# Weighing six of the twelve context chunks of a batch by three fp32r products of halves instead of plain fp32

## The chip, the cores and the metric

The kernel runs on one core of one Trainium2 chip. Its time is the device time of one execution in microseconds (us): the median of three runs. The page and the rows below come from one further execution that the hardware profiler recorded. The engines are named as in the profile: PE is TensorE, DVE is VectorE, ACT is ScalarE, POOL is GpSimd, SP issues the DMAs.

## What is computed

One decoder layer on `x` (32 batches, 56 tokens, 128 wide), in three parts: a position attention whose weights come from a small LSTM, a cross attention to `ctx_1024` (32 batches, 1500 rows, 128 wide), and a feed-forward layer with four experts. The change lies in the cross attention:

```
def _L0_xattn_ref(Q, K, V, WQ, WK, WV, WO, bO):      # K = V = ctx_1024, 16 heads of 64
    q = (Q @ WQ).reshape(N, ql, HEADS, DK)
    k = (K @ WK).reshape(N, kl, HEADS, DK)
    v = (V @ WV).reshape(N, kl, HEADS, DV)
    compat = jnp.einsum('nqhk,nlhk->nhql', q, k) / math.sqrt(DK)
    weights = jax.nn.softmax(compat, axis=3)
    attn = jnp.einsum('nhqk,nkhv->nqhv', weights, v).reshape(N, ql, HEADS * DV)
    return attn @ WO + bO
```

## The kernel before

WQ with WK, and WV with WO, are folded into one 128x128 matrix a head, so that keys and values are the raw context. A batch has 16 heads x 56 tokens = 896 columns, taken in two halves of 448 (`HALF`), and its 1500 context rows are 12 chunks (`CH`) of 125 (`CR`). Batches go in pairs: `i` is the pair (16), `k` the batch in the pair, `b = 2i + k`.

For chunk `j` of a batch: ACT seeds the PSUM scores with minus the column's maximum (`seed`, L976); PE adds the scores to them by three fp32r products of halves for each 448 columns, high x high, low x high, high x low (`scores`, L717); ACT takes the exponential into `probs[j % 4]` (L1033); POOL adds the chunk into `prob_sum` (L447 for the first two chunks together, L452 for the others); PE weighs the context with it, `ctx_nat` as the stationary operand, in plain fp32 into `usum_ps` (`weigh`, L729). In the trace one plain fp32 product is two matmul instructions, and one fp32r product is one.

The order is written out by hand. PE's `period(i, k)` has 12 slots, one for each `j`. A slot is: scores of chunk j+1, first half; place 0; scores, second half; place 1; weighing of chunk j-1, first half; place 2; weighing, second half; place 3. In the places stands side work, given by the strings `PLACES`, one word a slot (the first row for k = 0, the second for k = 1): m is a 128x500 product for the next batch's column maxima (L598), which DVE reduces (`read_max`, L1252); d spreads the maxima (L603) after DVE has made `max_diag` (L1259); t turns a third of the next context (L590), which ACT and DVE split into halves (L898, L1139); q makes queries (L629); s is the sums (L609) and p the projection (L617) of the previous pair, read by DVE. Side work alternates between two PSUM banks, and a product waits until its bank has been read.

DVE goes through the same slots: `take_u` at j = 1, the reads of place 0, the low halves of turned context (`late_turns`), the reads of place 1, those of places 2 and 3. At j = 11 it makes `q_lo` (L1244) from `q_hi`, which ACT makes just before (`query_hi`, L963). ACT's order for a chunk is: exponential, the copies of side work of slot j-1 (`side_copies`), seed of chunk j+2. The last batch has side work of its own: the layer norm of the third part (L1099, with its power on POOL, L377), routing, and on POOL the halves of the first expert weights (`expert_halves`, L433 and L435).

```
PLACES = ("m..m mssm ssmm mmpm .mpm mmpm mmpm mqmm mqqt ..dd qt.. t...",
          "m..m mm.m mm.m mm.m m.m. m.m. m.mt m.m. m.mt ..dd .... .t..")
```

## Time and profile before

| | |
|---|---|
| median of three runs | 1722.85 us (1722.15 to 1723.15) |
| the profiled execution | 1721.62 us |
| its span, first to last instruction | 1719.5 us |
| PE busy | 1647.4 us, 96% of the span |
| DVE, ACT, POOL busy | 843.5, 918.7, 792.1 us |
| share of the chain that ended last | PE 87%, DVE 8%, ACT 2% |
| mean granted PE clock | 0.975 of full speed |

The chain is the sequence of work that ended last, followed back from the end; a piece of it is what the program really spent, whereas the record of a single matmul also covers the time in which the next is already running behind it. Some 1380 us of the span are the batches' loop, and every pair of batches looks like the one shown below (755.3 to 844.9 us).

### The profile page before, as it was taken

How to read it: one execution, taken by the hardware profiler on the slowest of the kernel's cores; microseconds unless marked ns; L12 is line 12 of the kernel's file. 1: busy time of each engine (PE TensorE's matmuls, PEld its weight loads, DVE VectorE, ACT ScalarE, POOL GpSimd, SP SyncE). 2: the span in 40 equal slices, each digit the busy share in tenths (PEclk: the TensorE clock that was granted, in tenths of full speed). 3: DMA queues.
4: the chain of work that ended last, by engine and by line, in shares of the span. 5: the costliest groups of instructions: out<-in, count | busy, mean ns of one | idle time of the engine just before them, and what ended most of it. 6: DMA issues, size and time to landing. Idle time of an engine off the chain costs nothing.

```text
span 1719.5 us, 25064 instructions
## 1 busy us (share of the span) xinstructions
PE 1647.4 (96%) x7783; PEld 1181.7 (69%) x7783; DVE 843.5 (49%) x1772; ACT 918.7 (53%) x1311; POOL 792.1 (46%) x414
## 2 busy tenths in 40 slices
PE   6876999999999999999999999999999999998997
PEld 3344677777777777777777777767677777776664
DVE  3349445454545444454545445454454545454345
ACT  3233565656565656555555556565656565655211
POOL 2003454545454555545455555454545454545410
PEclk9996899999999999999999999999999999999788
DMA  4000000000000000001010101000000000000000
GB/s 150 25 17 2 1 36 37 36 36 36 36 36 36 36 36 36 36 29 43 18 45 15 44 20 40 31 36 36 36 36 36 36 36 36 36 18 1 1 1 22
DMA packets 15052, 54.84 MB, mean 32 GB/s; under 512 B 919, under 2 KB 6122, under 8 KB 15022
## 3 DMA queue, kind: packets, MB, share of 16 engines
q1 hardware_dynamic: 15022, 54.46, 8.4%
q8 instruction: 17, 0.28, 0.1%
q14 instruction: 13, 0.11, 0.0%
HBM read 53.54 MB, written 0.92 MB: 32 GB/s over the span
## 4 chain that ended last, share of the span: by engine, by line
PE 87%; DVE 8%; ACT 2%; issue 1%; POOL 1%; DMA 0%; DVEq 0%; POOLq 0%; ACTq 0%
PE ps L729 32%; PE ps L717 26%; PE ps L598 9%; PE ps L617 3%; PE ps L629 3%; PE ps L779 3%; PE ps L609 3%; PE ps L590 2%; DVE max_diag L1259 2%; PE ps L524 1%; DVE max_parts L1252 1%; PE ps L603 1%; DVE xnorm L1099 1%; ACT arena L877 1%; ACT arena L880 1%
## 5 line engine op out<-in xcount | busy, mean ns | idle before, releaser
L452 POOL TENSOR_TENSOR arena<-arena,probs 125x896 f32<-125x896 f32 x320 | 677.6, 2118 | 546.8 <-ACT probs L1033 456.6
L729 PE MATMUL ps<-probs,ctx_nat 125*128 125x448 f32 x1536 | 685.7, 544 | 0.0
L1252 DVE TENSOR_REDUCE max_parts<-ps 128x1 f32<-128x500 f32 x672 | 451.6, 676 | 354.7 <-PE ps L598 347.2
L1033 ACT ACTIVATE probs<-ps 125x896 f32<-125x896 f32 x384 | 351.6, 916 | 474.3 <-PE ps L717 430.9
L598 PE MATMUL ps<-ctxT_hi,q_hi 128*128 128x500 f32 x672 | 365.1, 544 | 2.2 <-DVE max_parts L1252 1.3
L976 ACT ACTIVATE ps<-arena 125x896 f32<-125x896 f32 x384 | 354.1, 922 | 7.9
L729 PEld LDWEIGHTS ps<-probs,ctx_nat 125*128 125x128 f32 x1536 | 277.6, 191 | 95.8 <-issue 79.7
L717 PE MATMUL ps<-q_hi,ctxT_hi 128*125 128x448 f32 x768 | 331.2, 431 | 1.8 <-ACT ps L976 1.8
L717 PE MATMUL ps<-q_lo,ctxT_hi 128*125 128x448 f32 x768 | 282.8, 368 | 0.0
L717 PE MATMUL ps<-q_hi,ctxT_lo 128*125 128x448 f32 x768 | 281.7, 367 | 0.0
L717 PEld LDWEIGHTS ps<-q_hi,ctxT_hi 128*125 128x125 f32 x768 | 144.5, 188 | 70.0 <-issue 62.1
L598 PEld LDWEIGHTS ps<-ctxT_hi,q_hi 128*128 128x128 f32 x672 | 127.4, 190 | 82.2 <-DVE max_parts L1252 29.7
L717 PEld LDWEIGHTS ps<-q_lo,ctxT_hi 128*125 128x125 f32 x768 | 144.2, 188 | 42.5 <-issue 22.1
L717 PEld LDWEIGHTS ps<-q_hi,ctxT_lo 128*125 128x125 f32 x768 | 143.2, 186 | 14.2
L447 POOL TENSOR_TENSOR arena<-probs 125x896 f32<-125x896 f32 x32 | 68.4, 2139 | 149.0 <-ACT probs L1033 149.0
L1139 DVE TENSOR_TENSOR ctxT_lo<-ps,ctxT_hi 128x500 fp32r<-128x500 f32 x96 | 64.4, 670 | 131.0 <-ACT ctxT_hi L898 131.0
L1244 DVE TENSOR_TENSOR q_lo<-arena,q_hi 128x896 fp32r<-128x896 f32 x32 | 38.8, 1212 | 92.8 <-ACT q_hi L963 92.8
L898 ACT ACTIVATE ctxT_hi<-ps 128x500 fp32r<-128x500 f32 x96 | 56.3, 587 | 45.9 <-PE ps L590 45.9
L617 PEld LDWEIGHTS ps<-vo_w,arena 128*112 128x112 f32 x512 | 64.0, 176 | 23.8 <-issue 23.8
L1290 DVE SCALAR_TENSOR_TENSOR resid<-ps,sum_recip,resid 112x128 f32 (+1 forms) x128 | 44.3, 346 | 63.6 <-PE ps L617 63.6
L629 PEld LDWEIGHTS ps<-xT,qk_w 128*128 128x128 f32 x512 | 67.1, 196 | 11.0 <-issue 9.1
L629 PE MATMUL ps<-xT,qk_w 128*128 (+1 forms) x512 | 69.3, 281 | 0.6 <-ACT xT L859 0.6
(186 smaller groups left out, 1259.6 us busy)
## 6 DMA issues: line engine op xcount, KB each, us to landing
ctx_raw<-in_ctx_dram SPq DMA_DIRECT2D x32, 750.0 KB
ctx_nat<-in_ctx_dram SPq DMA_DIRECT2D x32, 750.0 KB
w_sb<-in_L_ffn_W_dram SPq DMA_DIRECT2D x1, 1024.0 KB
resid<-in_x_dram SPq DMA_DIRECT2D x1, 896.0 KB, 6.7
out_dram<-ctx_raw SPq DMA_DIRECT2D x4, 224.0 KB, 2.5
ctx_raw<-in_L_xattn_WQ_dram SPq DMA_DIRECT2D x1, 512.0 KB
w_sb<-in_L_xattn_WK_dram SPq DMA_DIRECT2D x1, 512.0 KB
w_sb<-in_L_xattn_WV_dram SPq DMA_DIRECT2D x1, 512.0 KB
```

The lines of the kernel that those rows point to most:

```text
L447: g.tensor_tensor(first_sum if k == 0 else summed, chunk[0], chunk[1], ALU.add).then_inc(s["prob_added"], 1)
L452: g.tensor_tensor(summed, first_sum if j == 2 and k == 0 else summed, chunk[j % NP], ALU.add).then_inc(s["prob_added"], 1)
L598: mm(ps[:, bank, 0:MC], q_hi[nk][:, block_ * 128:(block_ + 1) * 128], ctxT_hi[nk][:, part * MC:(part + 1) * MC], start=True, stop=True).th ...
L617: m = mm(ps[0:TOK, bank, n * D:(n + 1) * D], u_sum[:, h].rearrange("p b q -> p (b q)"), vo_w[:, h, :], start=True, stop=True)
L629: m = mm(ps[:, bank, n * TOK:(n + 1) * TOK], qk_w[:, 4 * which + n, :], xT[:, bass.ds(i + 1, 1), :].rearrange("p k t -> p (k t)"), start=T ...
L717: m = mm(score_ps[j % 2][:, half, :], cx[k][:, rows], q[k][:, cols], start=False, stop=True, skip_group_check=True)
L729: m = mm(usum_ps[:, half, :], ctx_nat[k][:, j, :], probs[j % NP][:, half, :], start=(j == 0), stop=(j == CH - 1))
L898: a(ctxT_hi[k][:, which * MC:(which + 1) * MC], ps[:, bank, 0:MC], ACT.Copy).then_inc(s["ctxT_hi_done"], 1)
L976: a(score_ps[j % 2], neg_max[k][0:CR], ACT.Copy).then_inc(s["seeded"], 1)
L1033: a(probs[j % NP][:], score_ps[j % 2], ACT.Exp, scale=SCALE).then_inc(s["prob_done"], 1)
L1139: v.tensor_tensor(ctxT_lo[k][:, part], ps[:, bank, 0:MC], ctxT_hi[k][:, part].bitcast(F32), ALU.subtract).then_inc(s["ctxT_lo_done"], 1)
L1252: v.tensor_reduce(max_parts[:, which:which + 1], ps[:, bank, 0:MC], AX.X, ALU.max).then_inc(s["max_read"], 1)
```

## The change

Chunks 1, 3, 5, 7, 9 and 11 (`SPLIT`) are weighed by three fp32r products for each 448 columns, `ctx_hi` x `p_hi`, `ctx_hi` x `p_lo`, `ctx_lo` x `p_hi`; the other six stay plain fp32. For this:

- ACT takes a second exponential of the same scores into `p_hi` (fp32r), behind the side copies and ahead of the seed of chunk j+2; the exponential into `probs` stays.
- DVE subtracts, `p_lo = probs - p_hi`, 125x896, between the reads of place 1 and those of places 2 and 3.
- POOL makes `ctx_hi` and `ctx_lo` of the next batch in three parts of two chunks each, behind its adds of chunks 4, 6 and 8: six instructions of 125x256 a batch. The first batch's are made ahead of the loop; in the last batch there are none.
- PE waits for `prob_lo_done` ahead of a split chunk, and for `ctx_lo_done` once a batch.
- `probs` moves into `arena` and `wo_raw`, two of the `onehotT` tiles into `ctx_hi[0]` and `ctx_lo[0]`.

```
+        SPLIT = (1, 3, 5, 7, 9, 11)
...
+            def context_halves(i, k, part):
+
+                nb, (c0, c1) = 2 * i + k, PARTS[part]
+                chunks, halves = slice(c0, c1 + 1, c1 - c0), slice(2 * part, 2 * part + 2)
+                need(pool, f"nat_in{k}", 16 * (i + 1))
+                need(pool, "weighted", CH * (nb - 1))
+                g.tensor_tensor(ctx_hi[k][:, halves, :], ctx_nat[k][:, chunks, :], ones[0:CR, None, :].to_broadcast((CR, 2, D)), ALU.mult).then_inc(s["ctx_hi_done"], 1)
+                need(pool, "ctx_hi_done", len(PARTS) * nb + part + 1)
+                g.tensor_tensor(ctx_lo[k][:, halves, :], ctx_nat[k][:, chunks, :], ctx_hi[k][:, halves, :].bitcast(F32),
+                                ALU.subtract).then_inc(s["ctx_lo_done"], 1)
...
+                    if j in PART_SLOTS and not (isinstance(i, int) and i == PAIRS - 1 and k == 1):
+                        context_halves(i + k, 1 - k, PART_SLOTS.index(j))
...
-                    need(pe, "prob_done", CH * b + j + 1)
-                m = mm(usum_ps[:, half, :], ctx_nat[k][:, j, :], probs[j % NP][:, half, :], start=(j == 0), stop=(j == CH - 1))
+                        need(pe, "ctx_lo_done", len(PARTS) * (b + 1))
+                    if j in SPLIT:
+                        need(pe, "prob_lo_done", split_count(b, j))
+                    else:
+                        need(pe, "prob_done", CH * b + j + 1)
+                if j in SPLIT:
+                    n = SPLIT.index(j)
+                    pairs = ((ctx_hi, p_hi), (ctx_hi, p_lo), (ctx_lo, p_hi))
+                    for m_, (cx, p) in enumerate(pairs):
+                        m = mm(usum_ps[:, half, :], cx[k][:, n, :], p[n % 2][:, half, :], start=(j == 0 and m_ == 0), stop=(j == CH - 1 and m_ == 2))
...
-                    a(probs[j % NP][:], score_ps[j % 2], ACT.Exp, scale=SCALE).then_inc(s["prob_done"], 1)
+                    a(probs[j % NP], score_ps[j % 2], ACT.Exp, scale=SCALE).then_inc(s["prob_done"], 1)
...
+                    if j in SPLIT:
+                        need(act, "weighted", free_half(b, j))
+                        a(p_hi[SPLIT.index(j) % 2], score_ps[j % 2], ACT.Exp, scale=SCALE).then_inc(s["prob_hi_done"], 1)
...
+                    if j in SPLIT:
+                        need(dve, "prob_hi_done", split_count(b, j))
+                        need(dve, "weighted", free_half(b, j))
+                        n = SPLIT.index(j) % 2
+                        v.tensor_tensor(p_lo[n], probs[j % NP], p_hi[n].bitcast(F32), ALU.subtract).then_inc(s["prob_lo_done"], 1)
```

DVE, the end of the batch with k = 1 of the first pair (it is written out ahead of the loop over pairs, in the same order as in the loop), from the maxima of slots 0 to 6 on, before:

```order
L1252 TENSOR_REDUCE max_parts<-ps 128x1 x16
L1139 TENSOR_TENSOR ctxT_lo<-ps,ctxT_hi 128x500
L1252 TENSOR_REDUCE max_parts<-ps 128x1 x3
L1256 TENSOR_REDUCE max_all<-max_parts 128x7
L1259 TENSOR_TENSOR max_diag<-ident,max_all 128x896
L1139 TENSOR_TENSOR ctxT_lo<-ps,ctxT_hi 128x500
L1244 TENSOR_TENSOR q_lo<-arena,q_hi 128x896
```

and after, from the subtraction of chunk 3 on:

```order
L1458 TENSOR_TENSOR p_lo<-wo_raw,p_hi 125x896
L1304 TENSOR_REDUCE max_parts<-ps 128x1 x4
L1458 TENSOR_TENSOR p_lo<-arena,p_hi 125x896
L1304 TENSOR_REDUCE max_parts<-ps 128x1 x4
L1191 TENSOR_TENSOR ctxT_lo<-ps,ctxT_hi 128x500
L1458 TENSOR_TENSOR p_lo<-wo_raw,p_hi 125x896
L1304 TENSOR_REDUCE max_parts<-ps 128x1 x3
L1308 TENSOR_REDUCE max_all<-max_parts 128x7
L1311 TENSOR_TENSOR max_diag<-ident,max_all 128x896
L1191 TENSOR_TENSOR ctxT_lo<-ps,ctxT_hi 128x500
L1458 TENSOR_TENSOR p_lo<-arena,p_hi 125x896
L1458 TENSOR_TENSOR p_lo<-wo_raw,p_hi 125x896
```

The maxima stand as they did; between them, in every odd slot, there is now one subtraction, and the last two of a batch stand around the ninth and eleventh chunk, behind `max_diag` and the turned context.

PE, in the loop at k = 1, a weighing in an even slot with the product for the maxima on either side, before:

```order
L717 MATMUL ps<-q_hi,ctxT_lo 125x448
L213 REGISTER_ALU
L598 MATMUL ps<-ctxT_hi,q_hi 128x500
L729 MATMUL ps<-probs,ctx_nat 128x448 x2
L213 REGISTER_ALU
```

and after, where `L221 ISA` is the wait for `prob_lo_done`:

```order
L634 MATMUL ps<-ctxT_hi,q_hi 128x500
L221 ISA
L773 MATMUL ps<-p_hi,ctx_hi 128x448
L773 MATMUL ps<-p_lo,ctx_hi 128x448
L773 MATMUL ps<-p_hi,ctx_lo 128x448
```

The two plain products (one a half of the columns) have become six, the second three of which read like the first and are left out above; in odd slots the two plain products stay.

## Rows read from the trace of the kernel before

**Rows 1.** The page, busy time, then PE and its clock in 40 slices.

```profile
PE 1647.4 (96%) x7783; PEld 1181.7 (69%) x7783; DVE 843.5 (49%) x1772; ACT 918.7 (53%) x1311; POOL 792.1 (46%) x414
...
PE   6876999999999999999999999999999999998997
...
PEclk9996899999999999999999999999999999999788
```

**Rows 2.** Windows: us, then PE, PEld, DVE, ACT, POOL busy (count), clock, DMA.

```profile
755.30:799.80 44.50, 44.24 (x174) 30.78 (x173) 21.86 (x30) 30.35 (x39) 25.32 (x12) 1.00 0.09 35
799.80:844.90 45.10, 45.10 (x235) 34.91 (x234) 22.28 (x47) 22.58 (x29) 21.24 (x10) 1.00 0.09 34
...
793.90:799.80 5.90, 5.90 (x26) 4.15 (x25) 1.35 (x1) 5.76 (x8) 3.04 (x2) 1.00 0.00 0
...
1559.80:1605.00 45.20, 36.20 (x144) 24.65 (x143) 22.53 (x45) 22.42 (x28) 30.24 (x18) 0.89 0.00 1
```

**Rows 3.** The chain, slot 5 of k = 1: start us, us, what.

```profile
777.04 0.23 PE ps L598
777.26 0.61 PE ps L717 x3
777.87 0.76 PE ps L729 x2
```

**Rows 4.** Groups of instructions: busy us, mean ns of one, idle before and releaser.

```profile
L452 POOL TENSOR_TENSOR arena<-arena,probs 125x896 f32<-125x896 f32 x320 | 677.6, 2118 | 546.8 <-ACT probs L1033 456.6 <-PE ps L609 88.5
```

**Rows 5.** The timeline of DVE: start us, us, instruction, idle before.

```profile
771.55 0.68 DVE L1252 TENSOR_REDUCE max_parts<-ps 128x1 f32<-128x500 f32 x1 [0.17 <-PE ps L598]
...
790.18 2.21 DVE L1259 TENSOR_TENSOR max_diag<-ident,max_all 128x896 fp32r<-128x896 f32 x1
...
798.16 1.35 DVE L1244 TENSOR_TENSOR q_lo<-arena,q_hi 128x896 fp32r<-128x896 f32 x1 [5.18 <-ACT q_hi L963]
...
835.83 1.09 DVE L1259 TENSOR_TENSOR max_diag<-ident,max_all 128x896 fp32r<-128x896 f32 x1
```

**Rows 6.** The timeline of POOL beside it.

```profile
772.47 2.10 POOL L452 TENSOR_TENSOR arena<-arena,probs 125x896 f32<-125x896 f32 x1 [1.38 <-ACT probs L1033]
...
789.33 2.10 POOL L452 TENSOR_TENSOR arena<-arena,probs 125x896 f32<-125x896 f32 x1 [1.33 <-ACT probs L1033]
...
796.46 2.11 POOL L452 TENSOR_TENSOR arena<-arena,probs 125x896 f32<-125x896 f32 x1 [1.63 <-ACT probs L1033]
...
836.58 2.29 POOL L452 TENSOR_TENSOR arena<-arena,probs 125x896 f32<-125x896 f32 x1 [2.34 <-ACT probs L1033]
```

**Rows 7.** The timelines of POOL and DVE in the last batch, where POOL is backlogged.

```profile
1594.43 1.27 POOL L435 TENSOR_TENSOR ctxT_lo<-w_sb,ctxT_hi 128x512 fp32r<-128x512 f32 x1
1595.66 4.36 POOL L452 TENSOR_TENSOR arena<-arena,probs 125x896 f32<-125x896 f32 x2
...
1595.85 1.96 DVE L1314 SCALAR_TENSOR_TENSOR arena<-arena 112x12 f32<-112x12 f32 x1
...
1598.06 2.00 DVE L1314 SCALAR_TENSOR_TENSOR arena<-arena 112x12 f32<-112x12 f32 x1
```

**Rows 8.** The chain around `max_diag` at k = 1, and in the last batch.

```profile
790.18 2.22 DVE max_diag L1259
...
792.54 0.45 PE ps L603
...
795.15 1.50 PE ps L729 x4
796.66 1.22 PE ps L717 x6
...
1566.71 5.42 DVE xnorm L1099 x4
```

**Rows 9.** The timeline of ACT at the end of k = 1.

```profile
794.55 0.92 ACT L976 ACTIVATE ps<-arena 125x896 f32<-125x896 f32 x1
795.41 0.90 ACT L1033 ACTIVATE probs<-ps 125x896 f32<-125x896 f32 x1
```

More of the change, by code:

```diff
@@ L91, in decoder_layer @@
         ctx_nat = [sb(f"ctx_nat{n}", [CR, CH, D]) for n in range(2)]
+        ctx_hi = [sb(f"ctx_hi{n}", [CR, NS, D], F32R) for n in range(2)]
+        ctx_lo = [sb(f"ctx_lo{n}", [CR, NS, D], F32R) for n in range(2)]
         ctxT_hi = [sb(f"ctxT_hi{n}", [D, L], F32R) for n in range(2)]
@@ L95, in decoder_layer @@
         q_lo = [sb(f"q_lo{n}", [D, HQ], F32R) for n in range(2)]
-        probs = [sb(f"probs{n}", [CR, 2, HALF]) for n in range(NP)]
+        p_hi = [sb(f"p_hi{n}", [CR, 2, HALF], F32R)[:] for n in range(2)]
+        p_lo = [sb(f"p_lo{n}", [CR, 2, HALF], F32R)[:] for n in range(2)]
         max_diag = sb("max_diag", [128, HQ], F32R)
@@ L116, in decoder_layer @@
         neg_max = [cut(HQ).rearrange("p (a b) -> p a b", a=2) for n in range(2)]
-        cut(3 * HQ)
+        probs = [cut(HQ, CR).rearrange("p (a b) -> p a b", a=2) for n in range(NP - 1)] + [
+            wo_raw[0:CR].rearrange("p f n -> p (f n)")[:, 0:HQ].rearrange("p (a b) -> p a b", a=2)]
         prob_sum = cut(2 * HQ, CR).rearrange("p (h b q) -> p h b q", h=H, b=2)
@@ L187, in decoder_layer @@
         b1_r = sb("b1_r", [E, 2, FF], F32R)
-        onehotT = [sb(f"onehotT{q}", [E, GT], F32R)[:] for q in range(GROUPS)]
+        spare = NS * D // GT
+        onehotT = [half[0:E].rearrange("p c d -> p (c d)")[:, n * GT:(n + 1) * GT] for half in (ctx_hi[0], ctx_lo[0]) for n in range(spare)]
+        onehotT += [sb(f"onehotT{q}", [E, GT], F32R)[:] for q in range(len(onehotT), GROUPS)]
         xT_halves = max_diag[:].rearrange("p (n t) -> p n t", n=2)
```

21 lines of the change are left out of this document (18 added, 3 removed).

## The prediction

> **What bounds the kernel now.** I read the page first. PE is busy 96% of the span and its clock is granted nine tenths or more in nearly all slices [rows 1]; the reader is to see that PE, at its full clock of 2.4 GHz, fills the loop. The windows over one pair of batches, the first with the batch k = 1 and one slot more, the second with most of k = 0, show it exactly: PE busy 44.24 us of 44.50 and 45.10 of 45.10, while ACT has 30.35 and 22.58, DVE 21.86 and 22.28, POOL 25.32 and 21.24 [rows 2]. So in the loop a nanosecond taken from PE is a nanosecond of the end, as long as nobody else comes late. The last batch is different: PE is busy only 36.20 of 45.20 us there [rows 2], and the chain runs over POOL and DVE [rows 8].
>
> **What one split weighing gives.** The chain gives the real price of each product, free of overlaps. Three fp32r products of 448 columns (the scores, L717) take 0.61 us, also where six of them take 1.22; one plain fp32 weighing of 448 columns (L729, two instructions) takes 0.76, or 0.75 where two of them take 1.50 [rows 3, 8]. Operands, columns and bank type of the new triple are those of the scores, except that the moving operand has 125 partitions and the stationary one 128 columns where the scores have 128 and 125. I take 0.755 - 0.61 = 0.145 us for each half of a chunk. There are 6 chunks x 2 halves x 32 batches = 384 of them: 384 x 0.145 = 55.7 us. Of these 12 lie in the last batch, where PE waits anyway; I count them at nothing: 372 x 0.145 = 53.9 us. Bounds for one half: 0.12 (a triple that costs 0.635, a little over 0.2 us a product) to 0.16.
>
> Against the rows stands a rule. The Trainium skill, "FP8 and Floating Point Precision", section TensorE Precision Notes, says that true FP32 makes four passes through the array. By it the change would save one pass of four, a quarter of 0.755, or 0.19 us a half and 73 us in all; the rows say 0.145, since an fp32r product takes 0.203 us and not 0.189. The sum goes by the rows.
>
> **What it adds, and under what it lies.**
> ACT: one exponential a split chunk, at the pace of one every 0.86 us (0.92 long, starts at 794.55 and 795.41 [rows 9]): 6 x 0.86 = 5.2 us a batch, to 30.35 + 5.2 = 35.5 of some 43 us at k = 1 and 27.8 at k = 0. It lies under PE, except at the end of k = 1, where ACT is already busy 5.76 of 5.90 us [rows 2] and two of the new exponentials (chunks 9 and 11) fall. ACT runs ahead there by more than a microsecond (the seed of the next batch's chunk 0 is done at 795.47, its scores begin at 796.66 [rows 8, 9]), so of 1.7 us more most is covered. Behind the new exponential are queued the seed of chunk j+2 and, at j = 11, `q_hi`; PE waits for both. Price: 0 to 0.6 us a pair; I take 0.1.
> DVE: one subtraction of 125x896 from two SBUF tiles. The nearest row is `max_diag`, 1.09 us, alone [rows 5]: 6 x 1.0 = 6 us a batch, to 28 of some 43. What is queued behind it are the reads of places 2 and 3, and so the banks of PE's side work.
> POOL: six instructions of 125x256. The nearest rows are 1.27 us for 512 columns [rows 7] and 2.12 for 896 [rows 4], on a line through which 256 columns take 0.7: 4.2 us a batch. With that POOL has 29.5 us of some 43 at k = 1. Behind them wait its adds, and for those only the ring of four `probs`, three slots later, and the sums of the next pair.
>
> **The wait that the change adds.** The timelines of DVE and POOL side by side show that the two do not overlap when a DVE instruction reads two SBUF tiles. `max_diag` started at 790.18 while POOL's add of 789.33 ran until 791.43; it ended at 792.39, 0.96 after it, and took 2.21 instead of 1.09. `q_lo` at 798.16 ended 0.94 after the add that ended at 798.57. At 835.83 DVE was first, and it was POOL's add that took 2.29 instead of 2.10 [rows 5, 6]. (The Trainium skill, "SBUF — State Buffer", section "SBUF: two separate sides", calls this an exclusive lock held for the whole instruction; by that rule, the trace agrees, these three cases to 0.02 us.) `p_lo` is such an instruction, so each costs DVE 1.0 us when it is first and up to 2.1 + 0.96 = 3.1 us when an add has just begun.
>
> Who is first? At k = 1, slot 3, DVE's second maximum starts at 771.55 and ends at 772.23; `p_lo` would follow. POOL's add of the next chunk starts at 772.47 [rows 5, 6]. `p_lo` wins by 0.24 us, and then the add is late by 0.7, which costs nothing. In slots 5 and 7 at k = 1 there is no maximum in place 1: `p_lo` is ready about 0.9 us earlier and meets the end of the previous add, which the new halves push back by 1.4 us; it waits 0 to 2 us. A slot of k = 1 is 4 pieces of PE for scores and weighing and two or three maxima: 2 x 0.61 + 2 x 0.755 + 2 or 3 x 0.23 = 3.2 or 3.4 us [rows 3]. The weighing of chunk j is due one slot after the scores that stand in slot j; POOL's next add begins an exponential of 0.92 us [rows 9] and two hand-overs after those, some 1.3 us by an estimate. Between POOL instructions a waiting DVE instruction gets its turn: in the last batch the DVE instructions at 1595.85 and 1598.06 ended at 1597.81 and 1600.06, each with the end of one of two adds that ran back to back [rows 7]. So `p_lo` waits for one add and not for a train. At k = 0 the slots are 4.1 us on average (a pair of 89.6 us, 755.3 to 844.9, less twelve of 3.3), and DVE has room. The tightest place is chunk 9 at k = 1: `max_diag`, the turned context and `p_lo` stand in a row on DVE against two adds, and slot 10 has no side work ahead of the weighing. There I expect a stall of 0 to 1 us a pair; `max_diag` itself already makes PE wait there (it ends at 792.40, PE goes on at 792.54 [rows 8]). I take 0.5 us a pair for all of these together, 15 x 0.5 = 7.5 us with ACT's share in it; bounds 0 and 2 us a pair, 0 and 30 us.
>
> The last batch: `p_lo` stands on DVE ahead of the layer norm, whose four scalings already take 5.42 us on the chain because they wait for POOL [rows 8], and later ahead of the routing. Six times 1 to 3 us, of which some lie in gaps: 0 to 10 us, I take 4. The halves of the first batch are made ahead of the loop while POOL idles: nothing. The move of `probs` into other tiles costs nothing that a row would show.
>
> **Sum**, against the profiled execution of 1721.62 us: 1721.6 - 53.9 + 7.5 + 4 = 1679.2. That execution is 1.2 us under the median, so the median becomes 1680.4. **Forecast 1680 us**, with 0.145 between 0.12 and 0.16 and stalls between 0 and 12 us: 1663 to 1694.
>
> **Rivals.**
> A. The stalls are larger, 1 to 2.5 us a pair: some `p_lo` meet adds in slots 5, 7 and 9 of k = 1, or ACT's two exponentials at its end come late. For it: both engines at 80% and more there. Price 15 to 38 us: 1688 to 1710.
> B, the other side. **`p_lo` loses the race in every odd slot.** The margin in slots 1 and 3 is 0.24 us. If `p_lo` regularly comes second, it ends 2.1 + 0.96 = 3.1 us after the add began, or 1.3 + 3.1 = 4.4 us after the scores of its slot; the weighing is due after 3.2 to 3.4, or about 4.1 at k = 0. That is 1.1 us a split chunk at k = 1 and about 0.2 at k = 0, and the maxima read late behind it hold PE's side work for as much again: 6 x 2.2 + 6 x 0.4 = 15.6 us at worst, 7.8 without the second part. It decides at 3.5 us a pair, where the gain is gone. Price with 7 us: 1723 + 16 x 3.5 = 1779; I call it 1725 to 1790. Against it: a slot that is held longer gives POOL time to finish, so that the next `p_lo` finds it idle.
> C. The change does not bring the faster products, since `ctx_hi` as stationary and `p_hi` as moving operand cost more than in the scores: at 0.25 us a product nothing is left on PE (0.75 against 0.755), and 1723 + 11 = 1734. For it speaks nothing in the rows.
>
> **Chances.** Forecast 0.58; A 0.26; B 0.11; C 0.02; better than 1663 (PE also loses the wait for `max_diag` and the smaller ones) 0.03. The range has to hold 8 in 10: the forecast's own and A up to 1706 give 0.80: 1663 to 1706. A measurement of this kernel tells 0.2% (3.4 us) from no change. Faster by more than that: forecast, A, better, and little of B: 0.87; within: 0.02; slower: 0.11.
>
> **What would show it.** The chain in an even slot: the split weighing at 0.61 us and an unchanged 0.75 in odd slots; a pair of 86.2 to 87.0 us instead of 89.6. `p_lo` with a median of 1.1 us in DVE's rows and a maximum near 3; if its median is 2 or more, B holds. PE's idle time ahead of the split weighing: under 0.5 us a pair. ACT's list of waits without PE behind it at the end of k = 1. The last batch, from the last pair's second batch to the end of its scores, 45 to 52 us instead of 45.2. It would be wrong by its first step if the triple took over 0.65 us, and by its second if DVE's wait for POOL sat on the chain of every slot.

## The result: 1682.38 us, 2.4% faster, 2.4 us over the forecast

The changed kernel took 1682.38 us (median of 4, 1678.46 to 1683.91); the kernel before took 1723.0 us on the same chip (1722.15 to 1723.47). The ratio is 0.9761, with a 95% interval of 0.9729 to 0.9794. The forecast was 1680 us, the range 1663 to 1706. Every ratio below is to runs of the kernel before on the chip of the run itself.

The profiled execution of the changed kernel is the one of 1678.46 us, with a span of 1676.7 us. Its page, busy time first, answers to [rows 1]:

```profile
PE 1604.0 (96%) x8167; PEld 1250.0 (75%) x8167; DVE 1094.7 (65%) x1964; ACT 1070.4 (64%) x1503; POOL 1002.1 (60%) x606
...
PEclk9997899999999999999999999999999999999698
...
PE 89%; DVE 5%; ACT 2%; issue 2%; POOL 1%; DMA 0%; DVEq 0%; POOLq 0%; ACTq 0%
```

PE has 43.4 us less to do and is still busy for 96% of the span; the others have gained 152 to 251 us each and lie beside it. The last line is the chain by engine: 89% of it is PE.

Two windows over the batches, us, then PE, PEld, DVE, ACT, POOL busy (count), clock, DMA; they answer to [rows 2]. The first is one pair of batches, the second the end of a pair:

```profile
776.87:863.62 86.75, 86.65 (x432) 69.97 (x431) 59.43 (x90) 62.38 (x79) 59.48 (x35) 1.00 0.09 35
732.40:776.90 44.50, 44.50 (x205) 35.53 (x204) 29.28 (x37) 36.31 (x47) 33.58 (x19) 1.00 0.09 35
```

PE still has next to no idle time, so what the kernel lost and gained in the loop can be read from how long a pair takes. I measure it by the issues of the load of `ctx_nat`, one a batch; between two of them that are ten pairs apart lie, in the kernel before and then in the changed one (SyncE's queue: start us, us, instruction):

```profile
354.68 0.26 SPq L342 DMA_DIRECT2D ctx_nat<-in_ctx_dram  x1
...
1250.88 0.26 SPq L342 DMA_DIRECT2D ctx_nat<-in_ctx_dram  x1
```

```profile
347.08 0.26 SPq L362 DMA_DIRECT2D ctx_nat<-in_ctx_dram  x1
...
1214.98 0.26 SPq L362 DMA_DIRECT2D ctx_nat<-in_ctx_dram  x1
```

That is 89.62 us a pair before and 86.79 us now. "The pair" of every run below is measured so.

The chain of the changed kernel in slots 3 to 5 and 8 of k = 1, answering to [rows 3]. L773 is the split weighing, L775 the plain one, L753 the scores, L634 a maximum product, L639 the spread of `max_diag`:

```profile
754.78 0.62 PE ps L773 x3
755.40 0.23 PE ps L634
755.63 0.61 PE ps L773 x3
...
757.70 0.75 PE ps L775 x2
758.46 0.22 PE ps L634
758.68 0.76 PE ps L775 x2
...
764.25 0.76 PE ps L775 x2
765.01 0.47 PE ps L634
765.48 0.75 PE ps L775 x2
...
771.53 0.20 PE ps L639
```

A split half costs 0.61 or 0.62 us and a plain one 0.75 or 0.76, so a half saves 0.14. Two more things are to be seen. The maximum product at 765.01 takes 0.47 where its neighbour takes 0.22: PE waited for its bank. That is no doing of the change, since the same product takes 0.48 in the kernel before (at 785.45). But ahead of the spread stands no `max_diag` any more, which in [rows 8] held PE up.

VectorE's `p_lo` and `max_diag` at k = 1, and GpSimd beside them, answering to [rows 5, 6]:

```profile
752.25 1.08 DVE L1458 TENSOR_TENSOR p_lo<-wo_raw,p_hi 125x896 fp32r<-125x896 f32 x1
...
757.72 2.12 DVE L1458 TENSOR_TENSOR p_lo<-arena,p_hi 125x896 fp32r<-125x896 f32 x1
...
769.58 1.17 DVE L1311 TENSOR_TENSOR max_diag<-ident,max_all 128x896 fp32r<-128x896 f32 x1
```

```profile
752.57 2.73 POOL L486 TENSOR_TENSOR arena<-arena 125x896 f32<-125x896 f32 x1 [1.09 <-ACT arena L1082]
755.26 0.75 POOL L456 TENSOR_TENSOR ctx_hi<-ctx_nat,ones 125x256 fp32r<-125x256 f32 x1
...
756.79 5.03 POOL L486 TENSOR_TENSOR arena<-arena 125x896 f32<-125x896 f32 x2
...
769.08 0.73 POOL L458 TENSOR_TENSOR ctx_lo<-ctx_nat,ctx_hi 125x256 fp32r<-125x256 f32 x1
769.76 2.95 POOL L486 TENSOR_TENSOR arena<-arena 125x896 f32<-125x896 f32 x1
```

At 752.25 `p_lo` is first, by 0.32 us; it takes 1.08, and GpSimd's addition takes 2.73 instead of 2.10. At 757.72 the addition is first, and `p_lo` takes 2.12. At 769.58 `max_diag` is first, because the context halves have put the addition off until 769.76; before, the addition was first there and `max_diag` took 2.21. The margin is small but steady: in all 14 pairs from 335 us on `max_diag` starts 0.18 to 0.20 us ahead of the addition. The groups of instructions (busy us, mean ns, idle before and releaser) of `p_lo`:

```profile
L1458 DVE TENSOR_TENSOR p_lo<-wo_raw,p_hi 125x896 fp32r<-125x896 f32 x96 | 141.7, 1476 | 55.2 <-ACT p_hi L1089 55.1
L1458 DVE TENSOR_TENSOR p_lo<-arena,p_hi 125x896 fp32r<-125x896 f32 x96 | 141.2, 1471 | 3.9 <-ACT p_hi L1089 3.1
```

### The profile page after: what moved, and what is told of

Read it like the earlier page. It is cut to its first block, busy times and chain, and to the rows that moved or that the text cites. A ratio compares the mean times of both kernels' runs of the same rounds, so it can differ in the third digit from the quotient of the medians.

```text
span 1676.7 us, 27332 instructions
## 1 busy us (share of the span) xinstructions
PE 1604.0 (96%) x8167; PEld 1250.0 (75%) x8167; DVE 1094.7 (65%) x1964; ACT 1070.4 (64%) x1503; POOL 1002.1 (60%) x606
## 4 chain that ended last, share of the span: by engine, by line
PE 89%; DVE 5%; ACT 2%; issue 2%; POOL 1%; DMA 0%; DVEq 0%; POOLq 0%; ACTq 0%
PE ps L753 28%; PE ps L775 17%; PE ps L773 14%; PE ps L634 10%; PE ps L665 4%; PE ps L653 3%; PE ps L825 3%; PE ps L645 3%; PE ps L626 2%; PE ps L560 1%; PE ps L639 1%; ACT arena L923 1%; PE ps L822 1%; ACT arena L926 1%; DVE max_parts L1304 1%
## 5 line engine op out<-in xcount | busy, mean ns | idle before, releaser
L486 POOL TENSOR_TENSOR arena<-arena 125x896 f32<-125x896 f32 x224 | 546.7, 2441 | 260.3 <-ACT arena L1082 168.9
L1082 ACT ACTIVATE arena<-ps 125x896 f32<-125x896 f32 x288 | 262.4, 911 | 184.1 <-PE ps L753 146.7
L775 PE MATMUL ps<-arena,ctx_nat 125*128 125x448 f32 x768 | 344.8, 545 | 1.1 <-issue 1.1
L634 PE MATMUL ps<-ctxT_hi,q_hi 128*128 128x500 f32 x672 | 315.9, 471 | 3.1 <-DVE max_parts L1304 1.3
L753 PE MATMUL ps<-q_hi,ctxT_hi 128*125 128x448 f32 x768 | 311.8, 406 | 1.8 <-ACT ps L1025 1.8
L753 PE MATMUL ps<-q_hi,ctxT_lo 128*125 128x448 f32 x768 | 281.8, 367 | 0.0
L753 PE MATMUL ps<-q_lo,ctxT_hi 128*125 128x448 f32 x768 | 281.2, 366 | 0.0
L486 POOL TENSOR_TENSOR arena<-arena,wo_raw 125x896 f32<-125x896 f32 x96 | 203.0, 2115 | 39.5 <-ACT wo_raw L1082 35.8
L1458 DVE TENSOR_TENSOR p_lo<-wo_raw,p_hi 125x896 fp32r<-125x896 f32 x96 | 141.7, 1476 | 55.2 <-ACT p_hi L1089 55.1
L753 PEld LDWEIGHTS ps<-q_hi,ctxT_hi 128*125 128x125 f32 x768 | 143.9, 187 | 44.7 <-issue 34.9
L634 PEld LDWEIGHTS ps<-ctxT_hi,q_hi 128*128 128x128 f32 x672 | 127.2, 189 | 65.8 <-DVE max_parts L1304 18.0
L1089 ACT ACTIVATE p_hi<-ps 125x896 fp32r<-125x896 f32 x192 | 175.7, 915 | 0.0
L775 PEld LDWEIGHTS ps<-arena,ctx_nat 125*128 125x128 f32 x768 | 138.4, 190 | 47.6 <-issue 39.6
L753 PEld LDWEIGHTS ps<-q_lo,ctxT_hi 128*125 128x125 f32 x768 | 143.5, 187 | 33.4 <-issue 12.1
L753 PEld LDWEIGHTS ps<-q_hi,ctxT_lo 128*125 128x125 f32 x768 | 142.6, 186 | 14.2
L773 PE MATMUL ps<-p_hi,ctx_hi 125*128 125x448 f32 x384 | 150.4, 392 | 0.4 <-DVE p_lo L1458 0.4
L481 POOL TENSOR_TENSOR arena<-arena 125x896 f32<-125x896 f32 x32 | 67.9, 2123 | 132.2 <-ACT arena L1082 132.2
L1458 DVE TENSOR_TENSOR p_lo<-arena,p_hi 125x896 fp32r<-125x896 f32 x96 | 141.2, 1471 | 3.9 <-ACT p_hi L1089 3.1
L773 PE MATMUL ps<-p_lo,ctx_hi 125*128 125x448 f32 x384 | 140.6, 366 | 0.0
```

The costliest lines, as they stand in the source:

```text
L481: g.tensor_tensor(first_sum if k == 0 else summed, chunk[0], chunk[1], ALU.add).then_inc(s["prob_added"], 1)
L486: g.tensor_tensor(summed, first_sum if j == 2 and k == 0 else summed, chunk[j % NP], ALU.add).then_inc(s["prob_added"], 1)
L634: mm(ps[:, bank, 0:MC], q_hi[nk][:, block_ * 128:(block_ + 1) * 128], ctxT_hi[nk][:, part * MC:(part + 1) * MC], start=True, stop=True).th ...
L753: m = mm(score_ps[j % 2][:, half, :], cx[k][:, rows], q[k][:, cols], start=False, stop=True, skip_group_check=True)
L773: m = mm(usum_ps[:, half, :], cx[k][:, n, :], p[n % 2][:, half, :], start=(j == 0 and m_ == 0), stop=(j == CH - 1 and m_ == 2))
L775: m = mm(usum_ps[:, half, :], ctx_nat[k][:, j, :], probs[j % NP][:, half, :], start=(j == 0), stop=(j == CH - 1))
```

## The experiments

**My theory** was that of the forecast: PE sets the pace, a split half saves 0.14 us, and some of it is given back where VectorE meets GpSimd's additions. **The rivals** were that the added work costs more or less than that (A, B), or that the gain has another source. The first four runs each do one part alone or leave one out.

**The products alone.** From the second batch on neither `p_hi` nor `p_lo` is made, and from the third on no context halves; PE waits for the plain exponential instead and multiplies what lies in the tiles.

```diff
-                    if j in SPLIT:
+                    if j in SPLIT and isinstance(b, int) and b == 0:
                         need(act, "weighted", free_half(b, j))
...
-                    if j in SPLIT:
+                    if j in SPLIT and isinstance(b, int) and b == 0:
                         need(dve, "prob_hi_done", split_count(b, j))
...
-                    if j in PART_SLOTS and not (isinstance(i, int) and i == PAIRS - 1 and k == 1):
+                    if j in PART_SLOTS and isinstance(i, int) and i == 0 and k == 0 and not (isinstance(i, int) and i == PAIRS - 1 and k == 1):
                         context_halves(i + k, 1 - k, PART_SLOTS.index(j))
```

> The changed kernel with its products alone: from the second batch on the second exponential, p_lo and (from the third) the context halves are not made, so six chunks of a batch are weighed with halves left from the first two batches. PE's program is that of the changed kernel. Theory (PE bound, 0.143 us a half of a chunk, and the rest of the changed kernel's time is stalls of 0.6 us a pair and the last batch): a pair of 86.2 us and 1667 us, between 1664 and 1671. Rival (the products alone save less and the added work costs nothing): 1678 to 1684, as the changed kernel.

It took 1678.29 us, a ratio of 0.974 (0.9701 to 0.9779), the pair 86.89 us. My theory missed (1664 to 1671): without any of the added work the kernel was no faster than with all of it. The time lies in the rival's range, but not for the rival's reason. The chain shows why (start us, us, what):

```profile
1116.77 2.36 DVE max_diag L1314
...
1119.26 0.45 PE ps L639
```

The wait for `max_diag` of [rows 8] is back. The group of `max_diag` here, and in the changed kernel:

```profile
L1314 DVE TENSOR_TENSOR max_diag<-ident,max_all 128x896 fp32r<-128x896 f32 x32 | 53.8, 1681 | 3.7
```

```profile
L1311 DVE TENSOR_TENSOR max_diag<-ident,max_all 128x896 fp32r<-128x896 f32 x32 | 36.7, 1147 | 3.7
```

**The added work alone.** All twelve chunks are weighed by plain fp32; halves, `p_hi` and `p_lo` are made and waited for.

```diff
-                if j in SPLIT:
+                if False:
                     n = SPLIT.index(j)
```

> The added work without the faster products: second exponential, p_lo, context halves and all waits as in the changed kernel, but all twelve chunks are weighed in plain fp32. Theory: the added work costs PE 0.6 us a pair in stalls and 2 us in the last batch, but slots are 0.28 us longer, so that part of the stalls is covered: 1724 to 1736 us, and p_lo keeps winning its race in slots 1 and 3. Rival (the added work costs nothing at all): 1723. Rival (the longer slots shift POOL's adds ahead of p_lo, and the race is lost): above 1745.

The profiled execution took 1721.85 us, the other three 1748.05 to 1751.56 us at a clock of 0.974 or 0.975, where the profiled one had 0.976. No ratio is drawn from this run, but its one trace holds both courses that a pair can take. From the second pair on nearly every pair takes 89.28 to 89.33 us by the loads; ten pairs that include one slower batch average 89.55. Two batches with k = 1 take 2.42 us more than the others (41.86 and 41.87 where they take 39.45). VectorE's `max_diag` in one of the usual pairs and in one of these two, and GpSimd beside it:

```profile
970.95 1.09 DVE L1311 TENSOR_TENSOR max_diag<-ident,max_all 128x896 fp32r<-128x896 f32 x1
...
1060.25 3.06 DVE L1311 TENSOR_TENSOR max_diag<-ident,max_all 128x896 fp32r<-128x896 f32 x1
```

```profile
970.95 3.04 POOL L486 TENSOR_TENSOR arena<-arena 125x896 f32<-125x896 f32 x1
...
1060.24 2.11 POOL L486 TENSOR_TENSOR arena<-arena 125x896 f32<-125x896 f32 x1
```

Both start within 0.01 us of each other in 14 of the 15 pairs from 256 us on, and within 0.02 in the other. (GpSimd's spans are rough in the profile, but VectorE's own, 1.09 or 3.06 us, leave no doubt about who came first.) In 13 of the 15 `max_diag` gets through in 1.09 us; twice the addition does, `max_diag` takes 3.06, and PE then waits for it and for the `p_lo` behind it. The other three executions are 26.2 to 29.7 us longer, which is what 11 or 12 more of the 13 meetings would cost if they were lost (an estimate from the 2.42 us). They have no trace, so that this is what happened in them is not shown. None of the three accounts fits: the race that was lost was that of `max_diag`, not that of `p_lo`. Where it was won the pair took 89.30 us, 0.3 less than before, since `max_diag` no longer waits; the added work still costs something, for with that wait taken away from the kernel before by itself the pair takes 89.11 (below).

**No subtraction on VectorE.** `p_lo` is not made after the first batch, and PE waits for `p_hi` instead.

```diff
-                    if j in SPLIT:
+                    if j in SPLIT and isinstance(b, int) and b == 0:
                         need(dve, "prob_hi_done", split_count(b, j))
```

> The changed kernel without DVE's subtraction from the second batch on (p_lo is left from the first batch; PE waits for p_hi instead). Theory (the stalls come from reads of side work that stand behind p_lo on DVE): most of the 0.6 us a pair and of the 2 us of the last batch come back, 1669 to 1674 us. Rival (ACT's second exponential makes the stalls): 1679 to 1683.

1671.94 us, ratio 0.9703 (0.9659 to 0.9747), pair 86.38, as the theory had it: without `p_lo` the pair is 0.41 us shorter.

**No context halves after the second batch.**

```diff
-                    if j in PART_SLOTS and not (isinstance(i, int) and i == PAIRS - 1 and k == 1):
+                    if j in PART_SLOTS and isinstance(i, int) and i == 0 and k == 0 and not (isinstance(i, int) and i == PAIRS - 1 and k == 1):
                         context_halves(i + k, 1 - k, PART_SLOTS.index(j))
```

> The changed kernel without POOL's context halves from the third batch on (the halves of the first two batches stay). Theory (they only lengthen POOL's trains, so that p_lo in slots 5, 7 and 9 waits longer): p_lo's mean falls from 1.47 to about 1.3 us, and 0 to 3 us come back, 1678 to 1683 us. Rival (POOL's backlog is what delays PE): 1670 to 1675.

1685.22 us, ratio 0.979 (0.9746 to 0.9833), pair 87.16. The intervals of this run and of the whole change overlap, but the pair is longer by 0.37 us although GpSimd does less. `p_lo` got shorter as expected (1.38 and 1.14 us on average for its two groups), so that was not it. The group of `max_diag` here:

```profile
L1312 DVE TENSOR_TENSOR max_diag<-ident,max_all 128x896 fp32r<-128x896 f32 x32 | 53.8, 1682 | 3.7
```

So a new theory: part of the change's gain has nothing to do with the products. GpSimd's halves stand in front of the addition that used to meet `max_diag`, and PE lost half a microsecond a pair to that meeting. The next two runs take the meeting away by itself.

**Before, with one wait more on GpSimd.**

```diff
                     need(pool, "prob_done", CH * b + j + 1)
+                    if k == 1 and j == 9 and not (isinstance(i, int) and i == PAIRS - 1):
+                        need(pool, "diag_done", b + 2)
```

> The kernel before, with one wait more: GpSimd's addition of chunk 9 in each odd batch waits until VectorE has written max_diag. All else is as before. Theory A (the 0.45 us that TensorE waits for max_diag each pair comes from VectorE meeting GpSimd's addition there, and the change got it back by pushing that addition later): max_diag takes 1.1 us in every batch (mean 1.1 where before shows 1.62), TensorE's wait for it goes, the pair of batches takes 89.1 to 89.2 us where before shows 89.62, and the kernel 1715 to 1717 us, a ratio near 0.996. Theory B (the wait only hides another one, or the held addition meets a later VectorE instruction that matters as much): the pair stays at 89.5 to 89.7 us and the time within 2 us of before.

1712.61 us, ratio 0.9966 (0.9945 to 0.9987), pair 89.11. Theory A held: one wait makes the kernel before faster by 0.34%, which the interval just tells from nothing; the pair, whose length repeats to 0.01 us from one ten pairs to the next, says it more surely. (The time lies under the one expected because the kernel before took 1718.62 us on this chip.) `max_diag` in it, by its duration min/median/max:

```profile
L1261 DVE TENSOR_TENSOR max_diag<-ident,max_all x32: 1091/1093/1094, 172.0 to 1542.6; 128x896 fp32r<-128x896 f32 x32
```

**The products alone, with the same wait** on top of the edits of the first run:

```diff
+                    if k == 1 and j == 9 and not (isinstance(i, int) and i == PAIRS - 1):
+                        need(pool, "diag_done", b + 2)
```

> The three fp32r products alone (no p_hi, no p_lo, no context halves after the first batches, as in the run of products alone), with the same one wait on GpSimd's addition of chunk 9 in odd batches. Part of the computation is left out, as there. Theory A: the products alone gained no more than the whole change because their max_diag still met GpSimd's addition; with it out of the way the pair of batches takes 86.3 to 86.5 us (86.89 without the wait), and the kernel about 1669 to 1672 us, a ratio near 0.969. Theory B: the pair stays at 86.8 to 87.0 and the kernel at 1677 to 1680.

1662.76 us, ratio 0.9683 (0.966 to 0.9705), pair 86.12, a little under what Theory A expected. With these two the 2.83 us that the change saves in a pair fall into three parts: the meeting of `max_diag` 0.51 (89.62 to 89.11), the products 3.00 (89.11 to 86.12, with rounding), and the added work, which gives back 0.67 (86.12 to 86.79). The first part depends on the rest: with the faster products the same meeting costs 0.77 us a pair (86.89 to 86.12).

**Without the second exponential.** From the second batch on `p_hi` is not made again, and `p_lo` waits for the first exponential.

```diff
-                    if j in SPLIT:
+                    if j in SPLIT and isinstance(b, int) and b == 0:
                         need(act, "weighted", free_half(b, j))
...
-                        need(dve, "prob_hi_done", split_count(b, j))
+                        need(dve, "prob_hi_done", split_count(b, j)) if isinstance(b, int) and b == 0 else need(dve, "prob_done", CH * b + j + 1)
```

> The whole change without the second exponential from the second batch on: p_hi keeps what the first batch left, and p_lo waits for the first exponential instead. Part of the computation is left out. Theory A (ScalarE's second exponentials lie beside TensorE and cost nothing, and p_lo comes 0.9 us earlier, before GpSimd's addition or just with it): p_lo's mean falls to 1.1 to 1.3 us and the time to that of the run without p_lo, ratio 0.970. Theory B (p_lo and the addition start together, so p_lo waits for it more often): p_lo's mean over 1.6 us, ratio 0.976 to 0.985. Were the second exponential itself on the path, ratio under 0.965.

1675.32 us, ratio 0.973 (0.9702 to 0.9758), pair 86.24. That is 0.3% under the change, with intervals that overlap. `p_lo` did not get shorter, 1.48 and 1.35 us on average, so neither account of `p_lo` was right; it started earlier, and what PE's weight loads waited for it fell from 4.0 to 2.6 us in the whole kernel. The difference of 0.55 us a pair is all that ScalarE's six exponentials a batch and the later start of `p_lo` behind them cost together.

**`p_lo` behind the reads of places 2 and 3**, so that it comes second.

```diff
                     side_reads(i, k, j, (1,))
+                    side_reads(i, k, j, (2, 3))
                     if j in SPLIT:
...
-                    side_reads(i, k, j, (2, 3))
```

> The whole change, with p_lo moved behind VectorE's reads of places 2 and 3, so that in slots 1 and 3 too GpSimd's addition starts first. Slot 3 of the changed kernel has p_lo from 752.25 to 753.33 and its weighing at 754.78, GpSimd's addition from 752.57. Theory A (the order on VectorE decides, p_lo has 1.1 to 1.5 us to spare): where p_lo loses, it ends near 755.8, 1.0 us too late, in slots 1 and 3 of each batch; 62 slots by 0.5 to 1.0 us are 31 to 62 us, so 1713 to 1745 us; p_lo's mean goes from 1.47 us to over 2.0. Theory B (VectorE has no read in most places, or TensorE's queue takes the lateness up): 1680 to 1690 us.

1784.69 us, ratio 1.0379 (1.0355 to 1.0402), pair 93.05: worse than either theory said. All instructions are the same as in the changed kernel; one of them stands a few places later on VectorE. The chain (start us, us, what), and who waited for `p_lo` in all:

```profile
802.44 0.24 PE ps L634
...
803.30 1.68 DVE p_lo L1459
805.03 0.87 PE ps L773 x3
...
809.81 2.66 DVE p_lo L1459
```

```profile
  PEld ps L773: 104.4, 81
  PE ps L773: 72.8, 81
```

`p_lo` starts only after the maximum read at 802.71, meets an addition, and PE stands still for it in 81 of 384 halves, 72.8 us in all and 104.4 counted from its weight loads. But `p_lo` did not get longer, as Theory A had it: its mean is 1.47 us, as in the change. It loses now at chunks 1, 3 and 5 of k = 1 (2.22, 1.67 and 2.65 us, where the change has 1.08, 1.08 and 2.12) and wins at 7, 9 and 11 (1.08 to 1.19, where the change has 1.49 to 2.42). PE waits for it at five chunks of a pair: 1, 3 and 5 of k = 1 (3.3 us together), and 3 and 5 of k = 0 (1.2 us), where `p_lo` is hardly longer than in the change (1.28 and 1.32 us, 1.27 and 1.08 there) and only starts later. So the run shows the price of a `p_lo` that comes late, by its later place and by the lost meetings together; only the part at k = 0 can be put down to the place alone. `max_diag` and `q_lo` come to meet an addition too: 2.03 and 1.75 us on average, against 1.15 and 1.09 in the changed kernel, and PE waits 11.3 us for the turned context behind `q_lo`.

**More chunks split**: sixteen a pair, 1 to 9 and 11 at k = 0.

```diff
-    SPLIT = (1, 3, 5, 7, 9, 11)
+    SPLIT = ((1, 2, 3, 4, 5, 6, 7, 8, 9, 11), (1, 3, 5, 7, 9, 11))
...
-        PART_SLOTS = (4, 6, 8)
+        PART_SLOTS = ((2, 3, 4, 6, 8), (4, 6, 8))
```

> Sixteen chunks of a pair by three products instead of twelve: in even batches chunks 1 to 9 and 11, in odd batches the odd ones as in the change; GpSimd makes the context halves of even batches in five places of the odd ones. 8 halves a pair more by 0.143 us are 1.14 us a pair, 18 us in 16 pairs. Theory A (TensorE sets the pace there as in the change): 1662 to 1670 us. Theory B (with a p_lo in every slot of even batches VectorE, at 65 per cent, and its waits for GpSimd come to set the pace): no gain or a loss, 1680 to 1720 us, with TensorE waiting for p_lo over 1 us a pair.

1747.81 us, ratio 1.0152 (1.0125 to 1.018), pair 90.86. Theory B held in its sign, though the time is above its range and the wait is not the one that it named. PE's waits by what released it (total us, times, longest us):

```profile
PE ps L642 <- DVE max_parts L1313: 27.5, 27, 4.3
PE ps L642 <- DVE ctxT_lo L1200: 19.4, 15, 1.3
...
PE ps L781 <- DVE p_lo L1467: 4.5, 17, 1.0
```

PE hardly waits for `p_lo` (1.77 and 1.59 us on average for its two groups), but for what is queued behind it on VectorE: maximum reads and the turned context. `q_lo` takes 2.09 us on average. One cause is not that of Theory B: the first of the five places for the halves lies in slot 2, and there GpSimd waits for the load of the context that it is to split (15 times, 43.9 us), as in no slot of the change; after it, in the pair from 868 us on, it works without a gap up to the end of the batch. Whether sixteen chunks would pay with the halves placed elsewhere was not tried.

**The additions held**, to remove the meetings that are left in the changed kernel. The context halves move ahead of the addition of their place.

```diff
+                    if not (isinstance(i, int) and i == PAIRS - 1 and k == 1):
+                        if k == 1 and j == 9:
+                            need(pool, "diag_done", b + 2)
+                        elif j in SPLIT:
+                            need(pool, "prob_lo_done", split_count(b, j))
```

> The whole change, with GpSimd's additions held: the addition of a split chunk waits until VectorE has made that chunk's p_lo, that of chunk 9 in odd batches until max_diag is written, and the context halves stand ahead of the addition of their place, so that they run while ScalarE makes p_hi. Theory A (what is left of the change's stalls, 0.6 us a pair, is p_lo waiting for an addition and the maximum reads behind it): p_lo takes 1.1 us in nearly every slot (mean 1.47 in the change), the pair takes 86.1 to 86.4 us (86.79 in the change) and the kernel 6 to 10 us less than the change, a ratio of 0.970 to 0.973. Theory B (the held additions come late themselves, to TensorE's column sums or to the buffers of the exponentials): the pair stays at 86.8 or grows, ratio 0.976 or more.

1712.43 us, ratio 0.994 (0.9918 to 0.9962), pair 88.85: Theory B, over 2 us a pair worse than the change. `p_lo` did get shorter (1.32 and 1.28 us), but a held addition runs later, and now it ran when `q_lo` was due (VectorE, then GpSimd):

```profile
880.31 1.16 DVE L1463 TENSOR_TENSOR p_lo<-wo_raw,p_hi 125x896 fp32r<-125x896 f32 x1 [3.98 <-ACT p_hi L1094]
882.04 2.35 DVE L1301 TENSOR_TENSOR q_lo<-arena,q_hi 128x896 fp32r<-128x896 f32 x1 [0.58 <-ACT q_hi L1014]
```

```profile
875.29 8.15 POOL L493 TENSOR_TENSOR arena<-arena 125x896 f32<-125x896 f32 x3
```

```profile
PE ps L639 <- DVE ctxT_lo L1196: 25.9, 30, 1.0
```

Three additions in a row end at 883.44, and `q_lo` 0.95 us after. PE waits for the turned context behind it at 30 batch ends, 25.9 us, or 1.7 us a pair. A long `q_lo` alone does not cost that: without the second exponential it takes 2.55 us at the ends of k = 1, and PE waits for nothing behind it. It is the late end that costs.

**Sixteen split, additions held**, both edits together:

```diff
+    SPLIT = ((1, 2, 3, 4, 5, 6, 7, 8, 9, 11), (1, 3, 5, 7, 9, 11))
...
+                        elif j in SPLIT[k]:
+                            need(pool, "prob_lo_done", split_count(b, k, j))
```

> Sixteen split chunks a pair (even batches 1 to 9 and 11) as in the run that took 1747.81 us, with the additions held as in the run beside it. Theory A (that run lost to p_lo waiting for additions, mean 1.77 us, and to the maximum reads behind it, and to nothing else): 8 halves a pair by 0.143 us come back, the pair takes 85.0 to 85.6 us, the kernel a ratio of 0.959 to 0.965. Theory B (with a second exponential and a p_lo in nine slots in a row ScalarE, VectorE and GpSimd have no room between two slots of 3.6 us whoever waits): ratio 1.00 or more, the time between 1715 and 1750 us.

1771.6 us, ratio 1.0287 (1.0258 to 1.0317), pair 92.46. Theory B held in its ratio, with a time above its range. Holding the additions made this one slower as well; `q_lo` takes 2.70 us on average, and PE waits 41.3 us for the turned context behind it. GpSimd waits for the load of the context here too (14 times, 20.1 us).

**Additions held, and that of chunk 11 until `q_lo` is made**, on top of the edit of the additions held.

```diff
+                        elif j == CH - 1 and not (isinstance(i, int) and i == PAIRS - 1):
+                            need(pool, "q_lo_done", b + 3)
                         elif j in SPLIT:
```

> As the run with the additions held, except that the addition of chunk 11 waits until VectorE has made q_lo, and not only p_lo. That run's pair took 88.85 us (86.79 in the change), with q_lo at 2.37 us on average (1.09 in the change), because the held additions came to run while q_lo was due, and TensorE waited 0.8 to 1.0 us for what VectorE does behind q_lo, at two batch ends a pair. Theory A (all of that loss is q_lo meeting an addition): q_lo takes 1.1 us, the pair 86.2 to 86.8 us and the ratio is 0.970 to 0.977. Theory B (holding GpSimd's additions costs by itself, q_lo only shows it): the pair stays at 88 us or more and the ratio over 0.985.

1699.43 us, ratio 0.9879 (0.9854 to 0.9903), pair 87.63: between the theories. It took back 1.22 of the 2.06 us a pair. `q_lo` is down to 1.09 us at the end of k = 0 and stays at 2.35 at the end of k = 1, where it now waits for the additions before chunk 11:

```profile
PE ps L641 <- DVE ctxT_lo L1198: 12.1, 15, 0.9
```

Half the waits are left, 0.8 us a pair, which is all but 0.04 us of the 0.84 by which this pair is longer than the changed kernel's. So the late `q_lo` explains most of the loss of the held additions; that freeing it at k = 1 too would bring a gain over the change was not tried. Of all versions that compute everything, the change itself remained the fastest.

## Why the prediction was right, step by step

**The price of a half** (0.145 us, 372 halves, -53.9 us). The price was right; what it brought was less. The chain can be summed by what PE does, over two pairs from 900 us on, each piece counted up to the start of the next (us a pair):

| | before, one wait more | products alone, same wait | whole without `p_lo` | whole without second exponential | whole change |
|---|---|---|---|---|---|
| weighings | 36.59 | 33.10 | 33.14 | 33.20 | 33.22 |
| maximum products | 9.80 | 10.04 | 10.03 | 10.09 | 10.33 |
| query products | 3.65 | 3.78 | 4.02 | 3.78 | 4.00 |
| all else | 39.08 | 39.20 | 39.20 | 39.18 | 39.25 |
| pair | 89.11 | 86.12 | 86.38 | 86.24 | 86.79 |

The weighings give 3.49 us a pair, 24 halves at 0.145. The other pieces take 0.49 of that back: the maximum products 0.24, by my account the shorter slot that VectorE has for its reads, the query products 0.13 and the rest 0.12 (why these do is not shown). So a half is worth 0.125 us in the pair, or 46.5 us in 15.5 pairs; by the ratios it is 0.9966 - 0.9683 = 0.0283 of 1723 us, 48.8 us, give or take 5.3. The term was mis-sized by 5 to 7 us: I let nothing come late behind a faster PE. The Trainium skill, "FP8 and Floating Point Precision", section TensorE Precision Notes, says four passes for true FP32, from which the prediction made an estimate of 73 us; the chain and the runs of the products alone agree on less.

**The meeting of `max_diag`.** The prediction named it, with its 0.45 us or so on the chain, and took it as something that stays, at "the tightest place". Here a step failed: I asked what the new halves on GpSimd would do to `p_lo`, not what they would do to the additions. They moved the addition from ahead of `max_diag` to behind it, by 0.2 us, and so 5.9 us came back (0.0034 of 1723, give or take 3.6; by the pair 15 times 0.51, 7.6 us) that the sum did not have. That they did so is luck: in the run of the added work alone the same two instructions start within 0.01 or 0.02 us of each other.

**The added work** (7.5 us in the loop, 4 in the last batch; bounds 0 and 40 together). Whole change less products, 0.9761 - 0.9683 = 0.0078, is 13.4 us, give or take 6.8 by the two intervals; in the loop it is 0.67 us a pair, 10 us, where 0.5 was taken. The table says where: the maximum products 0.29, behind `p_lo` or behind a later `p_lo`, since they fall back without either; the query products 0.22, which is the second exponential's, since they fall back only without it (PE waits 5.2 us for ScalarE's copies of them in the whole kernel, and 0.3 without it); the split and plain weighings 0.12. The prediction had 0.1 for ScalarE. Without `p_lo` the pair is 0.41 shorter and without the second exponential 0.55, together more than 0.67, since both shorten the same maximum products. The halves on GpSimd are not free either: without them the pair is 87.16 with the meeting of `max_diag` in it, and as that meeting costs 0.77 beside the faster products, some 86.4 by this estimate without it, against 86.79.

**The misses cancel**: -53.9 + 11.5 = -42.4 was forecast; -48.8 - 5.9 + 13.4 = -41.3 was found. The products brought 5 us less, the meeting that was not in the sum 6 us more, and that the total came out right to 1 us is luck. (The three found parts add up to the whole by how they are made, each run less the next; the whole is no check of them.)

**Readings and sums of the prediction that were off.** The three cases of the lock do not agree with "held for the whole instruction" to 0.02 us, but with each other: the instruction that has waited ends 0.96, 0.94 and, on GpSimd, 1.95 us after the end of the other, 0.13 to 0.15 us less than the 1.09 or 2.10 us that it takes alone. Rival A had "both engines at 80% and more" for it; by the prediction's own terms ScalarE has 35.5 of 43 us, but GpSimd 29.5 and VectorE 28, 69 and 65%. The upper end of the range, 1694, comes out only with the 4 us of the last batch added to the 12. And the 0.02 of rival C, at 1734 us, belongs to "slower" and not to "within".

**The race.** Predicted: `p_lo` first in slots 1 and 3 by 0.24 us; found: 0.32 in slot 3, and the addition late by 0.63 (0.7 predicted). Predicted: waits in slots 5, 7 and 9; found: it takes 2.12, 1.49 and 2.40 us there, and 2.39 in slot 11. Medians of 1.09 and 1.37 us and a longest of 3.01 lie where the prediction put them, and in the whole kernel PE's products waited 0.4 us for `p_lo` and its weight loads 4.0, under 0.3 us a pair together.

**GpSimd's halves** take 0.73 to 0.75 us alone, 0.7 predicted. **The pair** is 86.79, in 86.2 to 87.0. **The last batch**: from the last spread of the last pair's second batch to the end of its scores it takes 50.5 us (1510.71 to 1561.22) against 53.8 before (the window of 45.2 us in the prediction stopped short of the last scores), so it did not get longer there. What is behind the last scores did. The chain, where the experts' halves on GpSimd follow its last addition:

```profile
1561.25 0.93 ACT wo_raw L1082
...
1562.24 2.08 POOL arena L486
1564.32 2.10 POOL ctxT_hi L467
...
1566.50 1.54 POOL ctxT_lo L469
...
1568.28 0.65 PE ps L822 x2
```

From the last score to the experts' first product the chain runs over ScalarE and GpSimd for 7.06 us; before, it ran over PE's own weighing for 5.69 us. From the last spread to the end of the span the changed kernel takes 2.4 us more; 4 were taken, but for `p_lo` ahead of the layer norm and the routing, which is not where it was found.

**Rival A** (stalls of 1 to 2.5 us a pair) did not come: the added work gives back 0.67, though some `p_lo` meet additions in slots 5, 7 and 9, as it said. **Rival B** did not come either: `p_lo` wins slot 3 by 0.32 us. Its price, 1725 to 1790 us, holds the 1784.69 us of the run in which `p_lo` stands two reads later. Its mechanism is only half borne out: PE does stand still for `p_lo`, but at five chunks of a pair and not at all twelve, with an unchanged mean of `p_lo`, and `max_diag` and `q_lo` were not in it. My argument against it was that a longer slot gives GpSimd time to finish; in that run `p_lo` wins at chunks 7, 9 and 11 of k = 1 and loses at 1, 3 and 5. **Rival C** fell with the chain's 0.61 us.

## What to carry to other kernels

Where two engines can't work at the same time on certain instructions, the cost of a change is set by who comes first at a few places, and an addition, a move or a removal anywhere on either engine can turn that. Look for each such instruction on which the bounding engine waits (here `max_diag`, `q_lo` and, new, `p_lo`), and ask of every new instruction on the other engine which of these meetings it makes or undoes; one added wait was worth 0.34% in the kernel before, and one instruction a few places later cost 6%. Look at the margin as well: a meeting that starts within 0.01 us was won in 13 pairs of one execution and lost in two, and each loss cost 2.42 us. Faster work on the bounding engine pays less than its own price, since what stands behind it has a shorter slot (0.125 us for 0.145 here), and a part that is left out does not measure that part alone as long as such meetings exist.

## What the runs showed of the hardware

- VectorE's subtraction of two 125x896 SBUF tiles takes 1.07 to 1.09 us when GpSimd is idle or begins after it, and ends 0.94 to 0.96 us after the end of the addition that was ahead of it (`q_lo` at 882.04 with 2.35: 0.95). With three additions in a row GpSimd's own record shows one stretch of 8.15 us, and VectorE's instruction that was due before the last of them, `p_lo` at 880.31, got through in 1.16.
- Maximum reads (from PSUM) take 0.67 or 0.68 us beside GpSimd's additions and don't wait for them; they are late only when they are queued behind an instruction that does. The Trainium skill, "SBUF — State Buffer", section "SBUF: two separate sides", counts a VectorE instruction with two SBUF inputs among those that are locked out for a whole GpSimd instruction; by that rule, the trace agrees, both the waits of `p_lo`, `q_lo` and `max_diag` and the free reads.
- An fp32r product of 448 columns with a stationary operand of 125x128 and a moving one of 125 partitions costs PE 0.207 us on the chain of the changed kernel (72 of them 14.9 us a pair), nearly the 0.205 of the scores (144 of them 29.5 us).
- A program with the same instructions took 1721.85 us in one execution and 1748 to 1752 in three others at an equal clock (the added work alone). In the trace of the first, VectorE's `max_diag` and GpSimd's addition start within 0.02 us of each other in 15 pairs; twice the addition wins, `max_diag` takes 3.06 us instead of 1.09, and the batch is 2.42 us longer. The difference to the other three is 11 or 12 times that, an estimate; no trace of them shows it.
